# Gating loop of a graph layer on Trainium2: when the indices are fetched, and in which order VectorE takes the previous chunk

## What is computed

```python
h = (x_flat @ W_gat).reshape(M, HEADS, NUM_EXPERTS)          # 4 heads x 4
e = leaky_relu(a_src[src] + a_dst[dst], negative_slope=0.2)
e_max = segment_max(e, dst, num_segments=M)
ee = exp(e - e_max[dst])
denom = segment_sum(ee, dst, num_segments=M)
alpha = ee / (denom[dst] + 1e-16)
agg = segment_sum(h[src] * alpha[:, :, None], dst, num_segments=M)
```

## Time and profile before

| what | us |
|---|---|
| median of three runs | 2589.93 |
| lowest and highest of them | 2586.99, 2591.83 |
| the profiled execution | 2584.71 |
| its span in the trace | 2582.9 |
| first full turn of the loop begins (flags of chunk 1) | 1692.28 |
| loop's last full turn ends | 2411.15 |
| VectorE busy in the span | 1877.1 |
| GpSimd busy | 1718.3 |
| TensorE busy | 1157.9 |

### The profile page before, as it was taken

One profiled execution on the slowest core, in us unless ns is written; L12 is line 12 of the kernel. 1 busy time (PEld: TensorE's weight loads), 2 busy tenths in 40 slices (PEclk: granted clock), 3 DMA queues, 4 the chain that ended last, 5 costly groups with the idle time before them and its releaser, 6 DMA issues.

```text
span 2582.9 us, 33931 instructions
## 1 busy us (share of the span) xinstructions
PE 1157.9 (45%) x12439; PEld 974.0 (38%) x12439; DVE 1877.1 (73%) x3127; ACT 682.0 (26%) x696; POOL 1718.3 (67%) x1690
## 2 busy tenths in 40 slices
PE   4662000001011100100105597888888888888386
PEld 2221000001000000000004354488888888888366
DVE  8887679997979989884327301178888888888556
ACT  1110004434335443534101011222222222222221
POOL 0005777777777777777777577777777777677370
PEclk9775555555555555555555555589999999999658
DMA  9402113333323332334314325122222222222101
GB/s 347 180 1 70 50 61 104 103 100 100 99 88 106 108 93 91 101 100 133 101 29 47 73 68 131 24 26 26 39 28 26 41 26 26 41 26 26 29 10 34
DMA packets 138177, 187.94 MB, mean 73 GB/s; under 512 B 77628, under 2 KB 96254, under 8 KB 131438
## 3 DMA queue, kind: packets, MB, share of 16 engines
q1 hardware_dynamic: 83958, 122.34, 14.6%
q0 software_dynamic: 54080, 63.61, 13.9%
HBM read 98.53 MB, written 87.32 MB: 72 GB/s over the span
## 4 chain that ended last, share of the span: by engine, by line
POOL 39%; DVE 24%; PE 17%; issue 15%; ACT 1%; DMA 1%; DVEq 0%; SPq 0%; POOLq 0%; ACTq 0%
POOL arena L739 36%; DVE arena L1379 12%; PE psum L1065 11%; DVE arena L1382 6%; POOL d_adseed L829 2%; DVE arena L1940 2%; PE psum L1026 2%; DVE arena L1989 2%; PE psum L1038 2%; POOL d_qseed L763 2%; PE psum L1110 1%; PE psum L1141 1%; DMA arena<-in_x 1%; PE psum L1055 1%; DVE arena L1927 0%
## 5 line engine op out<-in xcount | busy, mean ns | idle before, releaser
L1379 DVE TENSOR_TENSOR arena<-arena 128x512 f32<-128x512 f32 (+17 forms) x1331 | 766.6, 616 | 214.9 <-DMA arena<-d_ac,arena 65.9
L739 POOL DMA_INDIRECT arena<-d_h,arena x668 | 644.8, 965 | 227.4 <-issue 200.6
L739 POOL DMA_INDIRECT arena<-in_kv,arena x640 | 663.1, 1036 | 195.1 <-issue 195.1
L1065 PE MATMUL psum<-arena 128*128 128x128 bf16 x10080 | 606.9, 223 | 84.6 <-DVEq L1987 83.1
L1065 PEld LDWEIGHTS psum<-arena 128*128 128x128 bf16 x10080 | 593.5, 100 | 89.2 <-DVE arena L1382 86.0
L862 PE MATMUL psum<-arena 128*128 128x128 f32 (+3 forms) x402 | 92.8, 401 | 1027.4 <-DVEq L1455 800.4
L862 PEld LDWEIGHTS psum<-arena 128*128 128x128 f32 (+3 forms) x402 | 70.9, 208 | 1050.4 <-DVEq L1455 815.8
L1382 DVE TENSOR_SCALAR arena<-arena 128x512 bf16<-128x512 f16 (+8 forms) x1067 | 336.3, 373 | 71.8 <-ACT arena L1285 21.3
L1379 DVE TENSOR_TENSOR arena<-psum,arena 128x512 f32<-128x512 f32 (+2 forms) x179 | 141.2, 796 | 209.4 <-PE psum L1026 202.6
L739 POOL DMA_INDIRECT arena<-d_adst,arena x40 | 54.3, 1358 | 220.9 <-DVEq L1626 209.0
L1026 PEld LDWEIGHTS psum<-arena 128*128 128x128 f32 x512 | 113.7, 328 | 146.8 <-issue 110.5
(11 more groups left out here) (190 smaller groups left out, 1485.6 us busy)
## 6 DMA issues: line engine op xcount, KB each, us to landing
d_gs<-arena SPq DMA_DIRECT2D x32, 768.0 KB
d_as<-arena SPq DMA_DIRECT2D x20, 1152.0 KB, 4.6
d_qseed<-arena SPq DMA_DIRECT2D x5, 4096.0 KB, 31.4
arena<-d_qseed SPq DMA_DIRECT2D x20, 1024.0 KB, 5.2
arena<-d_h,arena POOLq DMA_INDIRECT x668
arena<-in_kv,arena POOLq DMA_INDIRECT x640
d_adseed<-arena SPq DMA_DIRECT2D x1, 4096.0 KB, 29.2
arena<-in_w_blocks SPq DMA_DIRECT2D x1, 2304.0 KB, 20.1
```

What stands on the lines that cost most here:

```text
L739: return pool.indirect_dma_start(out, None, table, bass.IndirectOffsetOnAxis(index[:, t:t + 1], 0))
L1065: last = nc.tensor.matmul(ps[2 + turn_of(b, m)][:, k * PICK_W:(k + 1) * PICK_W], pick_hot[turn_of(b, m)][:, t, k * P:(k + 1) * P], h_split ...
L1379: return V.tensor_tensor(o, a_, b_, op)
```

## The change

SyncE waits for `g_laid` of chunk c-1 (its `lay` is done) instead of `g_used`, fetches indices and seeds at once, and waits for `g_rows_set` only ahead of the store, which comes after the fetches. On ScalarE `lay` moves ahead of `all_keys` 3 and `rows` behind `all_keys` 6. On VectorE `maximum` and `weighted_sums` are each cut in two, and the four parts (`edge_scores`, `maximum`, `messages`, `weighted_sums`) stand after pairs 0, 1, 2 and 3. `pick_keys` moves from ahead of the last two pairs to ahead of pair 4, that is between the long scan and `one_hot` 6. Nothing else is changed; each instruction on data is still there, once.

```diff
                     with sp.If(it * 2 + b < n_all):
-                        sp.wait_ge(g_used, it * 2 + (b - 1))
-                        sp.wait_ge(g_rows_set, it * 2 + (b - 1))
+                        sp.wait_ge(g_laid, it * 2 + (b - 1))
                         sp.sem_inc(waits_carried, 1)
-                        sp.dma_start(gout_v[...], g_rows[b]).then_inc(g_rows_out[b], 16)
...
                         sp.dma_start(ad_seed[b], gseed_v[...]).then_inc(ad_seed_in[b], 16)
+                        sp.wait_ge(g_rows_set, it * 2 + (b - 1))
+                        sp.sem_inc(waits_carried, 1)
+                        sp.dma_start(gout_v[...], g_rows[b]).then_inc(g_rows_out[b], 16)
...
                         all_keys(it, b, 2)
+                        lay(it, 1 - b, 1)
                         all_keys(it, b, 3)
-                        lay(it, 1 - b, 1)
                         all_keys(it, b, 4)
                         weigh(it, 1 - b, 1)
                         all_keys(it, b, 5)
+                        all_keys(it, b, 6)
                         rows(it, 1 - b, 1)
-                        all_keys(it, b, 6)
...
-            def maximum(it, b, back, first=False):
+            def edge_scores(it, b, back):
                 c1 = it * 2 + (b - 2 * back * b + 1)
                 dve.wait_ge(g_laid, c1)
...
                 link(it, b, back, V.scalar_tensor_tensor(x_, x_, 0.2, x_, ALU.mult, ALU.max))
+
+            def maximum(it, b, back, first=False):
                 if not first:
...
-            def weighted_sums(it, b, back):
+            def messages(it, b, back):
                 dve.wait_ge(g_weighed, it * 2 + (b - 2 * back * b + 1))
...
                 dve.sem_inc(g_used, 1)
+
+            def weighted_sums(it, b, back):
                 link(it, b, back, V.tensor_tensor_scan(g_sum, ...))
...
                         for m in range(BATCHES - 2):
+                            if m == BATCHES - 3:
+                                dve.sem_inc(waits_carried, 1)
+                                with dve.If(it * 2 + (b + 1) < n_all):
+                                    pick_keys(it + b, 1 - b)
+                                    dve.sem_inc(waits_carried, 1)
                             one_hot(it, b, m + 2)
                             take_picked(it, b, m)
-                            if m == 1:
-                                maximum(it, 1 - b, 1)
-                            if m == 2:
-                                weighted_sums(it, 1 - b, 1)
+                            if m < 4:
+                                (edge_scores, maximum, messages, weighted_sums)[m](it, 1 - b, 1)
                         for m in range(2):
                             dve.sem_inc(waits_carried, 1)
                             with dve.If(it * 2 + (b + 1) < n_all):
-                                if m == 0:
-                                    pick_keys(it + b, 1 - b)
                                 one_hot(it + b, 1 - b, m)
                             take_picked(it, b, BATCHES - 2 + m)
```

More of the change, by code:

```diff
@@ L700, in _ @@
                     with sp.If(it * 2 + b < n_all):
-                        sp.wait_ge(g_used, it * 2 + (b - 1))
-                        sp.wait_ge(g_rows_set, it * 2 + (b - 1))
+                        sp.wait_ge(g_laid, it * 2 + (b - 1))
                         sp.sem_inc(waits_carried, 1)
-                        sp.dma_start(gout_v[bass.ds(it * 2 + (b - 2), 1)].rearrange("c p j f -> (c p) j f"), g_rows[b]).then_inc(g_rows_out[b], 16)
                         nxt = it * 2 + b
@@ L710, in _ @@
                         sp.dma_start(ad_seed[b], gseed_v[bass.ds(nxt, 1)].rearrange("c p j f -> (c p) j f")).then_inc(ad_seed_in[b], 16)
+                        sp.wait_ge(g_rows_set, it * 2 + (b - 1))
+                        sp.sem_inc(waits_carried, 1)
+                        sp.dma_start(gout_v[bass.ds(it * 2 + (b - 2), 1)].rearrange("c p j f -> (c p) j f"), g_rows[b]).then_inc(g_rows_out[b], 16)
             sp.wait_ge(g_rows_set, n_all)
@@ L1997, in _ @@
             flags(0, 0, 0)
+            edge_scores(0, 0, 0)
             maximum(0, 0, 0, True)
+            messages(0, 0, 0)
             weighted_sums(0, 0, 0)
@@ L2034, in _ @@
                         flags(it, 1 - b, 1)
+                        edge_scores(it, 1 - b, 1)
                         maximum(it, 1 - b, 1)
+                        messages(it, 1 - b, 1)
                         weighted_sums(it, 1 - b, 1)
```

## The result

| | before | after |
|---|---|---|
| median, us (7 runs each) | 2589.76 | 2595.67 |
| lowest and highest | 2583.98, 2592.50 | 2593.59, 2601.41 |
| ratio after to before | | 1.0033, 95% interval 1.0019 to 1.0047 |
| the profiled execution (its span) | 2584.71 (2582.9) | 2594.60 (2592.8) |
| loop, flags of chunk 1 to those of chunk 16 | 718.87 | 730.48 |

The change makes the kernel about 0.3% slower. The loop is 11.6 us longer; in the profiled execution it began 2.8 us earlier and 1.1 us more lay behind it, which gives the 9.9 us between the two.

What follows compares the result with a forecast made beforehand. No engine was full; a cycle between VectorE and TensorE was taken to bound the loop, with VectorE nearly a bound. 13 x 0.86 - 0.86 - 2.4 = 7.9 us more on 2589.93 gave 2598, range 2574 to 2606.

Steps and rivals of the forecast that it cites:

- The sign and the mechanism: TensorE's idle stretch moves from pick 5 to pick 6, 4.2 us, and makes pick 6 cold; slower, chance 0.53.
- the indices: Rival at VectorE's keys: they still wait for indices, SP held by the store; 0.3 us a turn more, 2602; chance 0.04.
- the moved keys: Keys ahead of pair 4 on VectorE: an additional branch and two semaphore steps, taken as 0.3 us a turn.
- GpSimd: Rival in the loop: GpSimd was the bound, so its 26.8 us of index waits go, 2563; chance 0.04.
- VectorE's turn without waits: VectorE's own work in one new loop turn, summed from its parts and hand-overs: 46.4 us.
- The turn at full clock: Loop turn if pick 6 stays at full clock, VectorE waiting 0.6 at the last one-hots: 46.9 us, 0.86 less.
- The cold turn: Loop turn if the clock drops at pick 6, VectorE waiting 2.3 at the last one-hots: 48.65 us, 0.86 more.
- the 0.16 for links: Term in VectorE's new turn for four links between its parts: 0.16 us a turn.
- The last turn: Turn with no next chunk, from `one_hot` 4 to the next flags: 27.6 us where it was 30.0, 2.4 less.
- The sum: Whole kernel: 13 x 0.86 - 0.86 - 2.4 = 7.9 us more, giving 2598 on the median.
- one of the 14 turns was taken as warm: Pick 6 cold in 13 of 14 loop turns; the other stays at full clock and gains 0.86 us.
- the clock's rival: Rival ahead of pick 6: 4.2 us idle doesn't drop the clock, all 14 turns gain 0.86, 2576; chance 0.14.

Runs made afterwards that it cites:

- e4: Changed kernel with TensorE computing spread 0 of the next chunk 13 times over, ahead of pick 6: 2573.30 us, ratio 0.9945 to the kernel before.
- e1: Changed kernel with the next chunk's keys moved from ahead of pair 4 to ahead of pair 2: 2577.22 us, ratio 0.9959 to the kernel before.
- e5: Changed kernel with spread 1 of the next chunk ahead of pick 6 in TensorE's order: 2586.37 us, ratio 0.9998 to the kernel before.
- e3: Kernel before with SyncE's part of the change alone (early indices): 2584.18 us, ratio 0.9990 to the kernel before.
- e7: e3 with the keys moved ahead of pair 4, maximum and sums left in two pieces: 2584.16 us, ratio 0.9988 to the kernel before.
- e6: e4 with spread 1 of the next chunk ahead of pick 6 in TensorE's order: 2564.83 us, ratio 0.9923 to the kernel before.
- e9: Second profile of the changed kernel with the keys back at their old place, ahead of pair 5: 2597.48 us in one execution.

## Why the prediction was right

*The sign and the mechanism.* The idle stretch moved from pick 5 to pick 6 with 4.22 us where 4.2 was said, pick 6 went cold in every turn, pick 5 ran at 5.52 behind 1.25 (1.5 was said), and the wait at the last one-hots grew (2.45 in the mean, 2.04 above the bare branch of 0.41, where 2.3 was said). e4, e1 and e5 each take away one link of that and get time back. e3 and e7 clear the rivals: neither the indices, nor the moved keys, nor GpSimd.

*VectorE's turn without waits*, 46.4: e6, where it waits for nobody, has 46.51. *The turn at full clock*, 46.9: e4 has 47.06. Both were sums made of rows of before.

*The cold turn*, 48.65, against a mean of 48.66. This agreement is worth less than it looks: two errors cancelled. Three of the 13 turns began with something that the prediction doesn't have, a slow pick 0 (and the last turn with a fourth). Timeline of TensorE, then of VectorE, of after at the first of them:

```profile
1777.56 7.15 PE L1066 MATMUL psum<-arena 128*128 128x128 bf16 x96 [4.33 <-DVEq L1992]
1784.55 0.38 PE L1056 MATMUL psum<-arena 128*128 128x128 f16 x4
1786.88 0.40 PE L1056 MATMUL psum<-arena 128*128 128x128 f16 x4 [1.95 <-issue]
1787.11 7.15 PE L1066 MATMUL psum<-arena 128*128 128x128 bf16 x96
```

```profile
1794.30 2.55 DVE L1383 TENSOR_SCALAR arena<-arena 128x512 bf16<-128x512 f16 x8 [1.25 <-PE psum L1066]
```

Behind the 1.95 us in which TensorE goes round its loop, pick 0 ran at half clock as well, and `one_hot` 2, which needs its buffer, waited 1.25. Those three turns took 50.33, 49.95 and 50.41; the other ten took (632.58 - 150.69) / 10 = 48.19. So the term for a cold turn was 0.46 too big. In the turn from 1941.40 to 1989.38, 47.98 long, it can be taken apart: up to the start of `one_hot` 6 it took 30.35 where the prediction's terms make 30.82 (48.65 - 11.6 - 6.23), from there to the last one-hots 11.28 for 11.6, most of that since pick 6 started 3.16 behind `one_hot` 6 and not 3.38; the rest took 6.35 for 6.23. In the first part flags and the first pair took 4.89 (1941.40 to 1946.29) for 5.13, the last pair ahead of the scan 4.18 for 4.28, and the 0.16 for links didn't show; scan and keys took 5.84 for 5.72. Durations read from one turn of before were mostly a little long, and nearly all went into the sum with the same sign.

*The last turn*: -2.4 was said, -0.62 measured. The order of the work gave 1.5 of it: from `one_hot` 4 to the next flags it took 28.51 (2391.42 to 2419.93) for 30.0 before and the 27.6 of the forecast. What is missing is pick 6, which was cold there too (2408.72, 7.15 us behind 2.01 of idle time, where 5.6 was assumed). And a slow pick 0 had cost it 1.58 us at `one_hot` 2, where the kernel before waited 0.93.

*The sum.* 7.9 us were said; the loop grew by 11.6 in the profiled execution (13 turns at 0.87, the first 1.0 longer, the last 0.6 shorter), the medians by 5.9. The loop began 2.8 earlier in that execution, and the profiles of e1 to e9 have their first flags anywhere between 1690.98 and 1695.31, so a few us of that difference belong to the execution and not to the change. Two terms of the 7.9 were wrong by the same profile: one of the 14 turns was taken as warm, at -0.86, but all 14 were cold, and the last turn saved 1.8 less than said. That the median came within 3 us of 2598 is therefore in part luck. The stated range also ends at 2606, one below the 2607 that it says it takes in; nothing hangs on that here.

*What the clock's rival was judged by.* The prediction let one length decide, "between the 1.84 and 4.46 us that rows show". 4.2 fell on the side that was said, but the length of the last wait doesn't decide: pick 0 went cold behind 1.95 in after, pick 6 of the last turn behind 2.01, and pick 4 of e1 stayed at 5.52 behind 3.50, shown above. Before, the wait ahead of pick 0, 1.84 in the earlier trace rows and between 1.64 and 2.12 in the seven turns that have one, never slowed it. What besides the wait decides isn't settled by these runs.

## What to carry to other kernels

Where an engine waits inside a loop, the length of its wait is half of what matters; the other half is what follows it before the loop's limiting engine needs the result. Spreading out one engine's long work may push two other long pieces together, so lay the other engine's timeline beside the new order and see where its longest idle stretch comes to stand. If that stretch costs TensorE its clock, work without use in it can be cheaper than the wait: 48 idle matmuls a turn took 0.9% off the time of the changed kernel (2573.30 for 2595.67).

## What was not expected of the hardware

The half clock doesn't stay where the wait is. In the window that is shown above the granted share was still 1.00 through the 4 us without work and fell in the pick behind them. In after, 4 slow picks (at 1787.11, 1886.68, 2080.64 and 2371.17) came one pick later than the long wait, behind a second one of about 2 us that alone had slowed no pick 0 in the turns of the kernel before. And where the clock doesn't fall the turns are alike: in e4 and e6, at a share of 1.00 through the loop's middle, the 13 turns lie between 46.93 and 47.19 and between 46.20 and 46.64, where those of after go from 47.81 to 50.41.
